# One kernel of attention and mixture of experts: the preparation moves from a block of its own into attention's block

## The chip, the cores and the metric

The kernel runs on one core of one Trainium2 chip. The metric is the device time of one execution in microseconds. The kernel before takes 2116.58 us, the median of three runs between 2116.27 and 2116.94.

## The reference

For 16 batches of 512 tokens with 128 features (float32): six modulation rows come from a conditioning vector, then attention with 16 heads and a mixture of 8 experts, each behind a layer norm that is scaled and shifted by that modulation.

```python
mod = (_silu(c) @ wmod).reshape(B, 6, 1, -1)           # sa, ca, ga, sb, cb, gb
ga = (2 * (ga >= 0) - 1) * jnp.maximum(jnp.abs(ga), 0.25)   # gb likewise
h = _layernorm(x) * (1 + ca) + sa
x = x + ga * attention(h, W_Q, W_K, W_V, W_out, b_out) # causal softmax, 16 heads of 64
h = _layernorm(x) * (1 + cb) + sb
x = x + gb * experts(h, W1, b1, W2, b2, Wr, br)        # top 2 of 8, gelu
```

## The kernel before

The kernel is written as three blocks, one after the other; each block gives every engine its own list of instructions, and all engines meet at a block's end. The first block prepares. SP loads the first batch's x, c, b1, b2, wmod and the raw weights of q, k and v; POOL makes the identity, the mask and a row of -0.5, and loads the biases and the output's weights W_out (L206 to L211). TensorE transposes c, b1 and b2 (L220 to L222), VectorE copies them out (L250 to L252), silu of c is made (ACT L233, VectorE L255 to L257), six products with wmod give the modulation (L226, copied and incremented at L259 and L261), and eight small VectorE operations give the gates (L265 to L268). Each of the four weight matrices is then split in two parts: ACT rounds it to fp32r (hi, L237) and VectorE subtracts (lo, L273), since every product of the kernel is made as hi*hi + lo*hi + hi*lo.

The second block is attention. It handles a batch's 16 heads as eight pairs; the 16 batches are one body written out, a hardware loop of 14 turns, and one body written out. Ahead of the first pair stands a chain for batch 0: statistics (`ln_stats`, VectorE L653 and L657), the inverse deviation on POOL (`inv_std`, L330 and L333), the normalized rows (`ln_apply`, L665), four transposes (`h_transposes`, L383), scale and shift out of PSUM (`h_evac`, ACT L553, which reads the modulation), `round_h` and `rest_h` (ACT L588, VectorE L671), the projections of pair 0 (`project_q`, `project_k`, L357 to L359), their rounding (ACT L561 and L565) and the rests (`rest_q`, `rest_k`, VectorE L676 and L682). Then TensorE's queue holds for each pair, in this order: the scores (L410) in three units, in later pairs the weighted values (L451) and the transposes of the previous pair's probabilities (L436), the projections for the next pair, and two chunks of the values' projection (`values`). VectorE's queue holds the eight masks with their maxima (`mask_and_max`, L701), copies of transposed probabilities (L694), the rests of q and k for the next pair, and the inverse sums (`invert_sums`, L710), which release POOL's normalization (L347). ACT's queue holds the exponentials (L580), roundings, and copies of transposed probabilities and of values (`values_out`, L597).

The raw weights stand in `v_sb`, which the values overwrite from pair 0 (slots 0 and 1) and pair 1 (slots 2 and 3) on; the other temporaries of the preparation stand in `probs`. The third block is the mixture of experts. It uses the gates, b1, b2, Wr and br.

Of the kernel before, what the change touches and what calls it, by code (L numbers as in the profile page):

```python
# [12 lines left out]
P = 128  # L13
# [31 lines left out]
def adaln_moe_kernel(nc, resid, W_Q, W_K, W_V, W_out, b_out, W1, b1, W2, b2, Wr, br, c_in, wmod, out):  # L45
# [10 lines left out]
    with ExitStack() as ctx:  # L56
# [61 lines left out]
        with ExitStack() as pa:  # L118
# [29 lines left out]
            with ExitStack() as ps:  # L148

                raw_w = [v_sb[:, i, :] for i in range(3)]  # L150
                raw_wo = v_sb[:, 3, :]
                zv = probs[:, :, :, :].rearrange("p a b n -> p (a b n)")
                wmod_sb = zv[:, 0:6 * D]
                c_rows = zv[0:B, 1024:1024 + D]
                b1_rows = zv[0:E * HC, 1152:1152 + P]
                b2_rows = zv[0:E, 1600:1600 + D]
                c_cols = zv[:, 1280:1280 + B]
                e_c = zv[:, 1312:1312 + B]
                e1_c = zv[:, 1344:1344 + B]
                sig_c = zv[:, 1376:1376 + B]  # L160
                silu_c = zv[:, 1408:1408 + B]
                g_sign = [zv[:, 1440:1440 + B], zv[:, 1472:1472 + B]]
                g_mag = [zv[:, 1504:1504 + B], zv[:, 1536:1536 + B]]

                flat_w = [tuple(w[:, :] for w in pair_w) for pair_w in (wq, wk, wv)]
                flat_w.append(tuple(w[:, :, :].rearrange("p n d -> p (n d)") for w in wo))

                load_rows = sem("load_rows")
                load_w = [sem(f"load_w_{n}") for n in "qkvo"]
                w_rounded = sem("w_rounded")  # L170
                load_mod = sem("load_mod")
                load_kept = sem("load_kept")
                pool_zero = sem("pool_zero")
                pool_const = sem("pool_const")
                cols_ps = sem("cols_ps")
                exp_c = sem("exp_c")
                dve_chain = sem("dve_chain")
                cols_ok = sem("cols_ok")
                silu_ok = sem("silu_ok")
                mod_ps = sem("mod_ps")  # L180
                gates_ok = sem("gates_ok")

                with nc.Block() as block:
                    @block.sync
                    def _(sp):

                        sp.dma_start(x_all[:, 0:NT, :], resid[0].rearrange("(t p) d -> p t d", p=P)).then_inc(x_in, 16)
                        sp.dma_start(c_rows, c_in).then_inc(load_rows, 16)
                        sp.dma_start(b1_rows, b1.rearrange("e (c p) -> (e c) p", p=P)).then_inc(load_rows, 16)
                        sp.dma_start(b2_rows, b2).then_inc(load_rows, 16)  # L190
                        sp.dma_start(wmod_sb, wmod).then_inc(load_mod, 16)
                        for dst, src, load in zip(raw_w, (W_Q, W_K, W_V), load_w):
                            sp.dma_start(dst, src.rearrange("d h c -> d (h c)")).then_inc(load, 16)
                    @block.gpsimd
                    def _(pool):
                        pool.memset(ident[:, :], 0.0).then_inc(pool_zero, 1)
                        pool.memset(mask_w[:, :], 0.0).then_inc(pool_zero, 1)
                        pool.memset(neg_half[:, :], -0.5).then_inc(pool_const, 1)
                        pool.wait_ge(pool_zero, 2)
                        pool.affine_select(out=ident[:, :], in_=ident[:, :], compare_op=ALU.not_equal, fill=1.0,  # L200
                                           base=0, pattern=[[-1, P]], channel_multiplier=1).then_inc(pool_const, 1)

                        pool.affine_select(out=mask_w[:, 384:512], in_=mask_w[:, 384:512], compare_op=ALU.is_ge,
                                           fill=NEG, base=0, pattern=[[-1, P]], channel_multiplier=1)\
                            .then_inc(pool_const, 1)
                        pool.dma_start(bo_col[:, :], b_out.rearrange("(d o) -> d o", o=1)).then_inc(load_kept, 16)  # L206
                        pool.dma_start(br_b[:, :], br.partition_broadcast(P)).then_inc(load_kept, 16)
                        pool.dma_start(wr_sb[:, :], Wr).then_inc(load_kept, 16)
                        wo_v = W_out.rearrange("c (n two) d -> two c n d", two=2)
                        for half in range(2):  # L210
                            pool.dma_start(raw_wo[half * DH:(half + 1) * DH, :].rearrange("p (n d) -> p n d", n=NP),  # L211
                                           wo_v[half]).then_inc(load_w[3], 16)
                        pool.wait_ge(load_kept, 48)

                    @block.tensor
                    def _(pe):

                        pe.wait_ge(pool_const, 3)
                        pe.wait_ge(load_rows, 48)
                        pe.transpose(g_bank[:, 0:B], c_rows, ident[0:B, 0:B])  # L220
                        pe.transpose(g_bank[:, B:B + E * HC], b1_rows, ident[0:E * HC, 0:E * HC])
                        pe.transpose(g_bank[:, 64:64 + E], b2_rows, ident[0:E, 0:E]).then_inc(cols_ps, 1)  # L222
                        pe.wait_ge(silu_ok, 1)
                        pe.wait_ge(load_mod, 16)
                        for j in range(6):
                            mm = pe.matmul(s_banks[0][:, j * B:(j + 1) * B], wmod_sb[:, j * D:(j + 1) * D], silu_c,  # L226
                                           start=True, stop=True)
                        mm.then_inc(mod_ps, 1)

                    @block.scalar  # L230
                    def _(act):
                        act.wait_ge(cols_ok, 3)
                        act.activation(e_c, c_cols, ACT.Exp, scale=-1.0).then_inc(exp_c, 1)  # L233

                        for (hi, lo), raw, load, n in zip(flat_w, raw_w + [raw_wo], load_w, (1, 1, 1, 2)):
                            act.wait_ge(load, 16 * n)
                            act.activation(hi, raw, ACT.Copy).then_inc(w_rounded, 1)  # L237

                    @block.vector
                    def _(dve):  # L240
                        done = [0]

                        def link(ins):

                            done[0] += 1
                            ins.then_inc(dve_chain, 1)
                            dve.wait_ge(dve_chain, done[0])
# [64 lines left out]
            with nc.Block() as block:  # L312
# [41 lines left out]
                def _(pe):  # L354
# [130 lines left out]
                    def body(b, first, last):  # L485
# [4 lines left out]
                        for p in range(NP):  # L490
# [32 lines left out]
                            if now:  # L523
                                values(b, p, 0, now[0])
# [744 lines left out]
```

## Time and profile before

| what | us |
|---|---|
| median of three runs | 2116.58 |
| the profiled execution | 2116.83 |
| its span | 2115.0 |
| first block, up to the first instruction of the second | 19.5 |
| chain of batch 0, up to the first scores | 11.7 |
| attention, 16 batches | about 1318 |
| experts, 16 batches | about 766 |

The profile is of one execution. Times in the views are microseconds from the span's start. In a timeline row the first number is the start, the second the time taken, and in brackets stands how long the engine had been idle before and what released it. "PEld" is TensorE's load of weights beside the product. Matmul ends are modelled, so that the time between starts says more than the time of one.

### The profile page before, as it was taken

The numbers are of one execution on the slowest core, as the hardware profiler recorded it, in microseconds if no ns is written. First come the engines' busy times: TensorE is split into PE (matmuls) and PEld (weight loads), VectorE is DVE, ScalarE is ACT, GpSimd is POOL, SyncE is SP. The second block draws the span as 40 slices with busy tenths as digits, with TensorE's granted clock in tenths as the row PEclk, the third lists the DMA queues.
The fourth block names the chain that finished last, engine by engine and source line by source line (L and its number), as shares of the span: only waits on it lengthen the run. The fifth ranks groups of instructions, "written<-read, shape, count | busy, mean of one in ns | idle before, by whom it ended". The sixth has DMA issues, their size and how long they took to land. (4 is left out here: it accounts for less than half of the span.)

```text
span 2115.0 us, 46428 instructions
## 1 busy us (share of the span) xinstructions
PE 2016.3 (95%) x12751; PEld 1556.6 (74%) x12751; DVE 1691.4 (80%) x4517; ACT 1535.3 (73%) x3749; POOL 722.1 (34%) x1215
## 2 busy tenths in 40 slices
PE   4999999999999999999999999799999999999998
PEld 3777777777777776777777777478888888888887
DVE  5878777778778778778787787599888888988887
ACT  4878778778778777777777787477777777777775
POOL 2434443344443444343443443122222222222222
PEclk9999999999999999999999999899999999999999
DMA  3000000000000000000000000311111121111111
GB/s 108 21 1 1 0 0 0 0 0 0 0 0 0 0 0 0 0 0 0 0 0 0 0 1 1 113 48 51 45 45 45 56 69 50 50 45 45 45 59 37
DMA packets 41933, 49.46 MB, mean 23 GB/s; under 512 B 3177, under 2 KB 23713, under 8 KB 41889
## 3 DMA queue, kind: packets, MB, share of 16 engines
q1 hardware_dynamic: 41632, 48.41, 7.3%
q0 software_dynamic: 256, 0.53, 0.2%
q8 instruction: 20, 0.33, 0.1%
q14 instruction: 25, 0.20, 0.0%
HBM read 44.47 MB, written 4.46 MB: 23 GB/s over the span
## 5 line engine op out<-in xcount | busy, mean ns | idle before, releaser
L347 POOL TENSOR_SCALAR probs<-probs,rdenom 128x512 f32<-128x512 f32 (+3 forms) x1024 | 522.4, 532 | 742.3 <-DVE rdenom L710 742.3
L580 ACT ACTIVATE probs<-probs,neg_max 128x512 f32<-128x512 f32 (+3 forms) x1024 | 561.8, 550 | 204.8 <-DVE neg_max L701 204.8
L1027 ACT ACTIVATE hidden<-banks,b_cols 128x512 f32<-128x512 f32 x512 | 348.4, 685 | 198.5 <-PE banks L893 174.8
L701 DVE CUSTOM_DVE_ANT_0 probs<-banks,mask_w 128x512 f32<-128x512 f32 (+3 forms) x1024 | 433.5, 487 | 52.5 <-PE banks L410 50.5
L1146 DVE TENSOR_TENSOR hid_lo<-hidden,hid_hi 128x512 fp32r<-128x512 f32 x512 | 386.7, 763 | 67.7 <-ACT hid_hi L1035 55.4
L694 DVE COPY probs_T<-banks 128x512 f32<-128x512 f32 x384 | 262.2, 683 | 151.5 <-PE banks L436 149.6
L436 PE MATMUL banks<-ident,probs 128*128 128x128 f32 x2560 | 348.6, 275 | 0.5 <-DVE z_lo L714 0.5
L436 PEld LDWEIGHTS banks<-ident,probs 128*128 128x128 f32 x2560 | 293.4, 141 | 52.4 <-DVE neg_max L701 12.0
L965 POOL TENSOR_TENSOR acc<-acc,y_w 128x512 f32<-128x512 f32 x112 | 155.1, 1385 | 489.6 <-DVE y_w L1159 489.6
L451 PE MATMUL banks<-probs_T,v_sb 128*64 128x512 f32 (+3 forms) x2048 | 303.9, 439 | 10.4 <-DVE neg_max L701 5.4
L451 PEld LDWEIGHTS banks<-probs_T,v_sb 128*64 128x64 f32 x2048 | 139.1, 136 | 157.9 <-issue 123.3
L410 PE MATMUL banks<-k_hi,q_hi 64*128 64x512 f32 (+3 forms) x1024 | 184.4, 349 | 41.1 <-DVE k_lo L682 28.3
L891 PE MATMUL banks<-h_hi,w_hi 128*128 128x512 f32 x512 | 207.3, 405 | 3.6 <-DVE w_lo L1132 2.6
L904 PE MATMUL banks<-hid_hi,w_hi 128*128 128x512 f32 x512 | 199.9, 390 | 1.9 <-DVE w_lo L1132 1.9
L893 PE MATMUL banks<-h_lo,w_hi 128*128 128x512 f32 x512 | 201.0, 393 | 0.0
L892 PE MATMUL banks<-h_hi,w_lo 128*128 128x512 f32 x512 | 200.4, 391 | 0.0
L905 PE MATMUL banks<-hid_hi,w_lo 128*128 128x512 f32 x512 | 199.9, 390 | 0.0
L906 PE MATMUL banks<-hid_lo,w_hi 128*128 128x512 f32 x512 | 199.8, 390 | 0.0
L580 ACT ACTIVATION_READ_ACCUMULATOR probs<-probs,neg_max 128x1 f32 x1024 | 192.6, 188 | 0.0
L410 PEld LDWEIGHTS banks<-k_hi,q_hi 64*128 64x128 f32 x1024 | 100.4, 184 | 104.6 <-issue 69.4
L410 PE MATMUL banks<-k_hi,q_lo 64*128 64x512 f32 (+3 forms) x1024 | 169.6, 318 | 0.0
L410 PE MATMUL banks<-k_lo,q_hi 64*128 64x512 f32 (+3 forms) x1024 | 169.5, 319 | 0.0
(138 smaller groups left out, 3408.0 us busy)
## 6 DMA issues: line engine op xcount, KB each, us to landing
w_rows<-w_kept SPq DMA_DIRECT2D x128, 256.0 KB, 4.0
x_all<-in_L_attn_resid_dram SPq DMA_DIRECT2D x16, 256.0 KB, 2.8
out_dram<-y_result SPq DMA_DIRECT2D x16, 256.0 KB, 2.3
w_raw<-in_L_ffn_W_dram SPq DMA_DIRECT2D x12, 256.0 KB, 3.9
hidden<-in_L_ffn_W_dram SPq DMA_DIRECT2D x4, 256.0 KB, 5.8
v_sb<-in_L_attn_W_Q_dram SPq DMA_DIRECT2D x1, 512.0 KB, 5.2
v_sb<-in_L_attn_W_K_dram SPq DMA_DIRECT2D x1, 512.0 KB, 8.0
v_sb<-in_L_attn_W_V_dram SPq DMA_DIRECT2D x1, 512.0 KB, 11.4
```

Of the source, the lines that this page charges most:

```text
L347: pool.tensor_scalar(part, part, rdenom[:, p % 2, 4 * h + r:4 * h + r + 1], 1.0, ALU.mult, ALU.mult)\
L410: mm = pe.matmul(S_BANK[u][h][:, at:at + n], q[own, p % 2, rows], k[own, p % 2, 0:n], start=start, stop=stop)
L436: mm = pe.transpose(T_BANK[u][:, at:at + P], probs[:, p % 2, h, src:src + P], ident[:, :])
L451: mm = pe.matmul(z_bank[h * DH:(h + 1) * DH, c * P:S], v_sb[:, c, hc:hc + DH], probs_T[:, h, KEY_AT[c]:KEY_AT[c] + n], start=(c == 0), sto ...
L580: act.activation(part, part, ACT.Exp, bias=neg_max[:, p % 2, col:col + 1], scale=-1.0, accum_out=denom[:, p % 2, col:col + 1]).then_inc(p_ ...
L694: dve.tensor_copy(dst, src).then_inc(t_dve, 1)
L701: dve.tensor_tensor_reduce(out=probs[:, p % 2, h, at:at + n], in0=S_BANK[u][h][:, col:col + n], in1=mask_w[:, 512 - n:512], scale=-SCALE, ...
L891: pe.matmul(banks[:, c, :], w1_hi[:, e, cols], h2_hi[:, :], start=True, stop=False)
L892: pe.matmul(banks[:, c, :], w1_lo[:, e, cols], h2_hi[:, :], start=False, stop=False)
L893: pe.matmul(banks[:, c, :], w1_hi[:, e, cols], h2_lo[:, :], start=False, stop=True)\
L1027: act.activation(hidden[:, e % 2, c, :], banks[:, c, :], ACT.Gelu, bias=b1_cols[:, e * HC + c:e * HC + c + 1]).then_inc(hid, 1)
L1146: dve.tensor_tensor(hid_lo[:, e % 2, c, :], full, hi.bitcast(F32), ALU.subtract)\
```

## The change

The first block is gone and its instructions stand at the head of attention's lists, in another order. SP issues c first, then x, wmod, the weights of q, k and v, and b1 and b2 last. POOL makes its constants, then the inverse deviation of batch 0, and issues its DMAs behind that. TensorE transposes c, then the normalized rows, then makes the modulation, then the projections of pair 0, and then transposes b1 and b2. ACT rounds q's weights ahead of `h_evac`, k's behind `round_h`, v's behind `round_k`, and the output's at the end of pair 0. VectorE takes silu between the statistics and the normalized rows, and splits q's and k's weights ahead of `rest_h` and `rest_q`; in pair 0 it splits v's weights and makes the gates behind the masks, and splits the output's weights behind the inverse sums. New waits hold TensorE: for the b columns between the first two units of pair 0's scores, and ahead of the values in pair 0 and pair 1 for three and four split matrices. The temporaries move to the half of `probs` that pair 1 is the first to use. The core of the diff:

```diff
-                zv = probs[:, :, :, :].rearrange("p a b n -> p (a b n)")
...
-                with nc.Block() as block:
...
+            zv = probs[:, 1, :, :].rearrange("p b n -> p (b n)")
...
@@ sync
+                    sp.dma_start(c_rows, c_in).then_inc(load_c, 16)
+                    sp.dma_start(x_all[:, 0:NT, :], resid[0].rearrange("(t p) d -> p t d", p=P)).then_inc(x_in, 16)
+                    sp.dma_start(wmod_sb, wmod).then_inc(load_mod, 16)
+                    for dst, src, load in zip(raw_w, (W_Q, W_K, W_V), load_w):
+                        sp.dma_start(dst, src.rearrange("d h c -> d (h c)")).then_inc(load, 16)
+                    sp.dma_start(b1_rows, b1.rearrange("e (c p) -> (e c) p", p=P)).then_inc(load_b, 16)
+                    sp.dma_start(b2_rows, b2).then_inc(load_b, 16)
                     batches(sp, body)
@@ gpsimd
...
+                    pool.wait_ge(pool_const, 1)
                     inv_std(0)
+                    wo_v = W_out.rearrange("c (n two) d -> two c n d", two=2)
...
+                    pool.wait_ge(load_kept, 48)
@@ tensor, body
-                        if first:
-                            h_transposes(0)
-                            project_q(0, 0)
-                            project_k(0, 0)
...
                             scores(b, p, 0, begin, young)
+                            if begin:
+                                pe.wait_ge(b_ok, 1)
                             scores(b, p, 2, begin, young)
...
+                            if first and p < 2:
+                                pe.wait_ge(w_split, 3 + p)
                             if now:
                                 values(b, p, 0, now[0])
@@ tensor, ahead of the batches
+                    pe.wait_ge(pool_const, 3)
+                    pe.wait_ge(load_c, 16)
+                    pe.transpose(g_bank[:, 0:B], c_rows, ident[0:B, 0:B]).then_inc(c_ps, 1)
+                    h_transposes(0)
+                    pe.wait_ge(silu_ok, 1)
+                    pe.wait_ge(load_mod, 16)
+                    for j in range(6):
+                        mm = pe.matmul(s_banks[0][:, j * B:(j + 1) * B], wmod_sb[:, j * D:(j + 1) * D], silu_c,
+                                       start=True, stop=True)
+                    mm.then_inc(mod_ps, 1)
+                    pe.wait_ge(w_split, 1)
+                    project_q(0, 0)
+                    pe.wait_ge(w_split, 2)
+                    project_k(0, 0)
+                    pe.wait_ge(load_b, 32)
+                    pe.transpose(g_bank[:, B:B + E * HC], b1_rows, ident[0:E * HC, 0:E * HC])
+                    pe.transpose(g_bank[:, 64:64 + E], b2_rows, ident[0:E, 0:E]).then_inc(b_ps, 1)
@@ scalar
+                    def round_weights(i):
+                        (hi, lo), raw, load = flat_w[i], (raw_w + [raw_wo])[i], load_w[i]
+                        act.wait_ge(load, 32 if i == 3 else 16)
+                        act.activation(hi, raw, ACT.Copy).then_inc(w_rounded, 1)
+
+                    act.wait_ge(c_ok, 1)
+                    act.activation(e_c, c_cols, ACT.Exp, scale=-1.0).then_inc(exp_c, 1)
+                    round_weights(0)
+                    act.wait_ge(mod_ok, 1)
                     h_evac(0)
                     round_h(0)
+                    round_weights(1)
                     round_q(0, 0, False)
                     round_k(0, 0)
+                    round_weights(2)
...
                             if len(now) > 1:
                                 values_out(b, 1, now[1])
+                            if begin:
+                                round_weights(3)
@@ vector
+                    def split_weights(i):
+                        (hi, lo), raw = flat_w[i], (raw_w + [raw_wo])[i]
+                        dve.wait_ge(w_rounded, i + 1)
+                        dve.tensor_tensor(lo, raw, hi.bitcast(F32), ALU.subtract).then_inc(w_split, 1)
+
+                    def gates():
...
+                    dve.wait_ge(c_ps, 1)
+                    dve.tensor_copy(c_cols, g_bank[:, 0:B]).then_inc(c_ok, 1)
                     ln_stats(0)
+                    dve.wait_ge(exp_c, 1)
+                    link(dve.tensor_scalar(e1_c, e_c, 1.0, None, ALU.add))
+                    link(dve.reciprocal(sig_c, e1_c))
+                    dve.wait_ge(c_ok, 1)
+                    dve.tensor_tensor(silu_c, c_cols, sig_c, ALU.mult).then_inc(silu_ok, 1)
                     ln_apply(0)
+                    dve.wait_ge(mod_ps, 1)
+                    link(dve.tensor_copy(mod_cols[:, :, :].rearrange("p j b -> p (j b)"), s_banks[0][:, 0:6 * B]))
+                    link(dve.tensor_scalar(mod_cols[:, 4, :], mod_cols[:, 4, :], 1.0, None, ALU.add))
+                    dve.tensor_scalar(mod_cols[:, 1, :], mod_cols[:, 1, :], 1.0, None, ALU.add).then_inc(mod_ok, 1)
+                    split_weights(0)
                     rest_h(0)
+                    split_weights(1)
                     rest_q(0, 0)
                     rest_k(0, 0)
+                    dve.wait_ge(b_ps, 1)
+                    dve.tensor_copy(b1_cols[:, :], g_bank[:, B:B + E * HC])
+                    dve.tensor_copy(b2_cols[:, :], g_bank[:, 64:64 + E]).then_inc(b_ok, 1)
...
                             mask_and_max(b, p, 1, 1)
+                            if begin:
+                                split_weights(2)
+                                gates()
...
                             invert_sums(b, p)
+                            if begin:
+                                split_weights(3)
```

## Rows read from the trace of the kernel before

**Rows 1.** The page, parts 1 and 3: busy time; packets, MB, share of a queue.

```profile
PE 2016.3 (95%) x12751; PEld 1556.6 (74%) x12751; DVE 1691.4 (80%) x4517; ACT 1535.3 (73%) x3749; POOL 722.1 (34%) x1215
...
q8 instruction: 20, 0.33, 0.1%
```

**Rows 2.** Windows: one batch; width, busy us (instructions) by engine, clock, DMA share, GB/s.

```profile
216.27:298.18 81.91, 78.81 (x586) 58.68 (x585) 63.25 (x199) 61.78 (x179) 33.86 (x66) 1.00 0.00 0
```

**Rows 3.** Timeline: attn_T of batch 0 and of batch 13, made one batch later.

```profile
134.31 0.81 DVE L723 TENSOR_SCALAR attn_T<-banks,bo_col,gate_cols 128x512 f32<-128x512 f32 x1 [4.62 <-PE banks L472]
...
1199.23 0.81 DVE L723 TENSOR_SCALAR attn_T<-banks,bo_col,gate_cols 128x512 f32<-128x512 f32 x1 [4.86 <-PE banks L472]
```

**Rows 4.** DMA view, 0 to 40 us: count, KB, median us from issue to landing.

```profile
x_all<-in_L_attn_resid_dram SPq DMA_DIRECT2D x8, 256.0 KB, 2.7
...
v_sb<-in_L_attn_W_V_dram SPq DMA_DIRECT2D x1, 512.0 KB, 11.4
```

**Rows 5.** Timeline, first block: start, us, engine, line, operation, [idle before <-releaser].

```profile
0.74 0.44 SPq L187 DMA_DIRECT2D x_all<-in_L_attn_resid_dram  x1
...
1.24 0.49 SPq L188 DMA_DIRECT2D probs<-in_L_c_dram  x1
...
4.25 0.25 PE L220 MATMUL banks<-ident,probs 16*128 16x16 f32 x1 [4.25 <-DMA probs<-in_L_ffn_b_dram]
...
6.73 2.71 PE L226 MATMUL banks<-probs 128*128 128x16 f32 x12 [2.02 <-DMA probs<-in_L_wmod_dram]
8.31 1.06 ACT L237 ACTIVATE wq_hi<-v_sb 128x1024 fp32r<-128x1024 f32 x1 [2.98 <-DMA v_sb<-in_L_attn_W_Q_dram]
9.47 0.26 DVE L259 COPY mod_cols<-banks 128x96 f32<-128x96 f32 x1 [3.43 <-PE banks L226]
9.77 0.38 DVE L261 TENSOR_SCALAR mod_cols<-mod_cols 128x16 f32<-128x16 f32 x2
...
11.61 1.22 DVE L273 TENSOR_TENSOR wq_lo<-v_sb,wq_hi 128x1024 fp32r<-128x1024 f32 x1
```

**Rows 6.** Timeline, second block up to the first scores.

```profile
19.56 0.87 DVE L653 BATCH_NORM_STATS2 stats<-x_all 128x6 f32<-128x128 f32 x4 [0.53 <-PEq L183]
...
21.19 1.04 POOL L333 TENSOR_TENSOR rstd<-var_eps,neg_half 128x4 f32<-128x4 f32 x1
22.27 1.11 DVE L665 TENSOR_SCALAR xn<-x_all,meanvar,rstd 128x128 f32<-128x128 f32 x4 [1.55 <-POOL rstd L333]
...
23.44 1.12 PE L383 MATMUL banks<-ident,xn 128*128 128x128 f32 x4 [14.00 <-DVE xn L665]
24.59 0.78 ACT L553 ACTIVATE hf<-banks,mod_cols 128x512 f32<-128x512 f32 x1 [7.20 <-PE banks L383]
...
26.81 0.79 PE L357 MATMUL banks<-h_hi,wq_hi 128*128 128x512 f32 x1 [2.26 <-DVE h_lo L671]
...
28.25 0.63 PE L357 MATMUL banks<-h_hi,wk_hi 128*128 128x512 f32 x1
...
31.24 0.50 PE L410 MATMUL banks<-k_hi,q_hi 64*128 64x512 f32 x2 [1.50 <-DVE k_lo L682]
```

**Rows 7.** Timeline, end of pair 0 and start of pair 1.

```profile
37.10 0.69 DVE L676 TENSOR_TENSOR q_lo<-banks,q_hi 128x512 fp32r<-128x512 f32 x1 [1.36 <-ACT q_hi L561]
...
38.43 1.06 ACT L597 ACTIVATE v_sb<-banks 128x512 f32<-128x512 f32 x2
38.56 0.69 DVE L682 TENSOR_TENSOR k_lo<-banks,k_hi 128x512 fp32r<-128x512 f32 x1 [0.77 <-ACT k_hi L565]
...
39.36 0.50 PE L410 MATMUL banks<-k_hi,q_hi 64*128 64x512 f32 x2 [1.90 <-issue]
...
40.47 0.69 DVE L701 CUSTOM_DVE_ANT_0 probs<-banks,mask_w 128x512 f32<-128x512 f32 x1 [1.11 <-PE banks L410]
```

**Rows 8.** Windows, columns as in Rows 2: two stretches of pair 1.

```profile
40.40:43.75 3.35, 3.35 (x24) 3.13 (x21) 3.28 (x15) 2.54 (x9) 3.23 (x7) 0.50 0.29 83
43.75:48.08 4.33, 4.33 (x27) 3.53 (x27) 2.92 (x7) 4.33 (x14) 0.44 (x1) 0.99 0.23 66
```

More of the change, by code:

```diff
@@ new lines, in adaln_moe_kernel @@
+            raw_w = [v_sb[:, i, :] for i in range(3)]
+            raw_wo = v_sb[:, 3, :]
+            zv = probs[:, 1, :, :].rearrange("p b n -> p (b n)")
+            wmod_sb = zv[:, 0:6 * D]
+            c_rows = zv[0:B, 1024:1024 + D]
+            b1_rows = zv[0:E * HC, 1152:1152 + P]
+            b2_rows = zv[0:E, 1600:1600 + D]
+            c_cols = zv[:, 1280:1280 + B]
+            e_c = zv[:, 1312:1312 + B]
+            e1_c = zv[:, 1344:1344 + B]
+            sig_c = zv[:, 1376:1376 + B]
@@ new lines, in adaln_moe_kernel @@
+            silu_c = zv[:, 1408:1408 + B]
+            g_sign = [zv[:, 1440:1440 + B], zv[:, 1472:1472 + B]]
+            g_mag = [zv[:, 1504:1504 + B], zv[:, 1536:1536 + B]]
+            flat_w = [tuple(w[:, :] for w in pair_w) for pair_w in (wq, wk, wv)]
+            flat_w.append(tuple(w[:, :, :].rearrange("p n d -> p (n d)") for w in wo))
+            load_c, load_b = sem("load_c"), sem("load_b")
+            load_w = [sem(f"load_w_{n}") for n in "qkvo"]
+            w_rounded = sem("w_rounded")
@@ new lines, in adaln_moe_kernel @@
+            load_mod = sem("load_mod")
+            load_kept = sem("load_kept")
+            pool_zero = sem("pool_zero")
+            pool_const = sem("pool_const")
+            c_ps, b_ps = sem("c_ps"), sem("b_ps")
+            exp_c = sem("exp_c")
+            dve_chain = sem("dve_chain")
+            c_ok = sem("c_ok")
+            silu_ok = sem("silu_ok")
+            mod_ok = sem("mod_ok")
+            mod_ps = sem("mod_ps")
+            gates_ok = sem("gates_ok")
+            b_ok = sem("b_ok")
@@ L277, in adaln_moe_kernel @@
+            w_split = sem("w_split")
             qk_ps = sem("qk_ps")
@@ new lines, in gates @@
+                    def gates():
+                        for g, j in enumerate((2, 5)):
+                            raw, sign, mag = mod_cols[:, j, :], g_sign[g], g_mag[g]
+                            link(dve.tensor_scalar(sign, raw, 0.0, 2.0, ALU.is_ge, ALU.mult))
+                            link(dve.tensor_scalar(sign, sign, 1.0, None, ALU.subtract))
+                            link(dve.tensor_tensor(mag, raw, sign, ALU.mult))
+                            dve.scalar_tensor_tensor(out=gate_cols[:, g, :], in0=mag, scalar=GATE_MIN, in1=sign,
+                                                     op0=ALU.max, op1=ALU.mult).then_inc(gates_ok, 1)
```

127 lines of the change are left out of this document (20 added, 107 removed).

## The prediction

> **What bounds the kernel now.** I read the page first. TensorE is busy for 95% of the span [rows 1], so over the whole the kernel is bound by TensorE, and the windows of one batch of the loop say the same: 78.81 of 81.91 us [rows 2]. attn_T is written at 134.31 and, 13 turns of the loop later, at 1199.23 [rows 3], 81.92 us apart each time, so a batch does not depend on how the first one began. What is gained or lost ahead of the loop then reaches the end one for one. The change touches only what stands ahead of the loop and two pairs of the first batch, so the average says nothing on its price, and I read the timeline of that stretch.
>
> The first block has three things in a row in it. The loads: the last of the v weights lands 11.4 us after its issue, at about 15.4 [rows 4]. The modulation: its products run from 6.73 to 9.44, and the columns are ready at 9.77 + 0.38 = 10.15 [rows 5]. The splits: four times 1.22 us on VectorE [rows 5], of which the last two wait for v's load. The second block starts at 19.56 with the statistics, which need only x. x was issued at 0.74 [rows 5] and an x load takes 2.7 us [rows 4], so it had lain there since about 3.5. That is 16 us of waiting for nothing, and it is what the change can reach. From 19.56 a chain with no slack follows, in which every engine waits for the one before [rows 6], up to the first scores at 31.24: 11.7 us.
>
> **Up to the first scores.** I lay the chain of [rows 6] at the time when its inputs are there.
> - c is now first in SP's queue (issue at 0.74 in place of 1.24). Its landing is not shown alone; TensorE started on it at 4.25 only because it waited for b2 as well [rows 5], so with the 0.5 us by which it moves up 3.7 is an upper bound, and the transpose and the copy (0.17) fit ahead of x.
> - x is second: issue 1.24, landing 2.7 later, 3.95. Statistics start at about 4.05 in place of 19.56: 15.5 us earlier. Then POOL's rstd at 5.7, xn at 22.27 - 15.5 = 6.8, transposes from 7.95 to 9.05. The three silu operations stand in VectorE's queue between statistics and xn; VectorE idles 1.55 us there [rows 6] and they took 0.67 in the first block, so they are free.
> - TensorE makes the modulation behind the transposes: 9.05 + 2.71 [rows 5] = 11.8. Before, this ran beside other work; now it is in the chain. wmod had landed by 6.73 from a later place in the queue [rows 5], so its load is not what is late. Copy and the two increments: 10.15 - 9.47 = 0.68, so `h_evac` starts at 12.55 in place of 24.59. The lead shrinks from 15.5 to 12.0 us.
> - ACT has q's rounding (1.06) in front of `h_evac`. It started at 8.31 on q's landing [rows 5], so it ends by 9.4, 3 us ahead of time. VectorE splits q from 12.5 to 13.7; `rest_h` takes some 0.7 us, as a rest of 512 columns does [rows 7], ahead of the 26.81 at which q's products start [rows 6], so it is due at 26.06 - 12.0 = 14.0. Free.
> - k's rounding follows `round_h` on ACT, which ends where `rest_h` starts, at 14.0: so k is rounded at 15.1 and split at 16.4. `project_k` would be due at 28.25 - 12.0 = 16.2 [rows 6]. It waits 0.1 to 0.2 us: 0.15.
> - v's rounding (1.06) runs from 18.5 to 19.6 on ACT, ahead of the first exponential, which cannot be due before the first mask, some 1.1 us behind the first scores (40.47 - 39.36 in pair 1 [rows 7]). The b transposes take less than the 1.5 us that TensorE idles between `project_k` and the scores [rows 6]; the b copies (0.35 us on VectorE behind `rest_k`) are done 0.7 us ahead of the first mask. b1 and b2 stand behind v's weights in the queue, which land by 15.4 [rows 4]; TensorE gets to them at 17.9. Free, with 2 us of margin.
>
> Scores start at 31.24 - 12.0 + 0.15 = 19.4: **11.85 us earlier**. Bounds: x or c half a us later or earlier; if the two increments and waits cost nothing more, 12.5, if each of some ten new hand-overs costs 0.1 us more than counted, 10.9.
>
> **Pair 0 and pair 1** (in times of before, to be shifted). VectorE ends its masks at 37.10 - 1.36 = 35.74 [rows 7]. Split of v's weights, 1.23: 36.97. Gates, eight operations between the increments' end at 10.15 and the first split at 11.61 [rows 5], so 1.46, and some more for the split's wait, 1.5: 38.5. The rest of q, which ran at 37.10, is 1.4 late and ends at 39.2. The rest of k was due at 38.56 [rows 7], now 39.2 to 39.9, and the scores of pair 1 start 0.65 late, at 40.0. The values' products wait for the split and move 1.25 us back into TensorE's idle stretch before 39.36 (1.90 us [rows 7]); ACT's copies of them, which ended at 39.49 [rows 7], end 0.1 late. ACT then rounds the output's weights, 39.6 to 40.65, and VectorE splits them until 41.9. So the first mask of pair 1 starts at 41.95 in place of 40.47 [rows 7]: 1.5 us late on VectorE and ACT. TensorE is not held by that in full. In 40.40 to 43.75 its clock was granted at half, 1.2 GHz, and VectorE was busy 3.28 of the 3.35 us; from 43.75 to 48.08 TensorE and ACT are both full [rows 8]. VectorE has 1.4 us of idle time in the second stretch, which takes up some of the 1.5 us; I estimate that 0.9 reach the scores of pair 2. The bounds are 0.6 (only TensorE's lateness counts) and 1.5 (ACT's in full). I take **0.9**, nearer to the lower end, since TensorE, late by 0.65, is as full as ACT.
>
> Here the trace and a page weigh differently. The trace shows the clock at half for 3.35 us behind TensorE's idle 1.90 us [rows 7, 8], at a place where VectorE covered it. The Trainium skill ("TensorE: Matmul & The Clock Gate", section "What's actually happening") has a throttled default that activity lifts and idling brings back. By it, the change, which lengthens the waits of pair 0, invites the low level and may put it in another place. This agrees with the row; what it would do is the second rival.
>
> **Behind that** nothing changes: gates, b1 and b2 are read by later parts only, and the loop is the same. The next x loads follow b2 in SP's queue, beside the output's weights, which have until about 27.7. The meeting of the engines at 19.5 disappears inside the 15.5 us already counted.
>
> **Sum** against the profiled execution: 2116.83 - 11.85 + 0.9 = 2105.9. It lies 0.25 us above the median of the runs, so 2105.6 in terms of the median.
>
> **Rivals.**
> 1. *VectorE becomes the bound of the first pairs.* All of what is put in its queue counts: 1.23 + 1.5 + 1.23 + 0.35 = 4.3 us in place of 0.9. For it: VectorE's masks release both ACT and the transposes. Against: 1.36 + 0.77 us of idle time [rows 7]. 2116.6 - 11.85 + 4.3 = 2109.0. Chance 0.10.
> 2. *The clock falls in another place*, over the scores of pair 0 or over pair 2, where TensorE is full. 3.35 us at half [rows 8] do 1.7 us of work, so 1.7 us more: 2107.3. Chance 0.10.
> 3. *The b columns hold the scores.* TensorE stands at `load_b` with all scores behind it, and the output's weights take a share of the DMA. If b lands 4 us behind where v's did, at 19.4, the transposes, copies and second unit come some 1.5 us late: 2107.1. Against: everything ahead of it in the queue landed by 15.4 [rows 4], and the output's weights, which shared the DMA then, now start later. Chance 0.05.
> 4. *The first pairs take the added work for nothing*: 2104.7. Chance 0.08.
> 5. *The reordering does not do what it says*: x shares the DMA with what follows and lands with the last of the weights, at 15.4. Then the chain starts 4.1 us earlier and not 15.5, and with 0.9 lost the time is 2113.4, within 0.2%. Against: the 2.7 us of an x load [rows 4]. Chance 0.02.
> 6. *Slower: the turn of the loop costs more.* The loop's instructions stand at other addresses now, so a turn could meet a fetch that it does not meet today. There are 14 turns in each of the loops; TensorE's idle time in a whole batch is 81.91 - 78.81 = 3.1 us [rows 2], and a stall of up to that size per turn is conceivable. From 15.2 / 14 = 1.1 us per turn the kernel is over 0.2% slower; at 1.2 us per turn it takes 2105.6 + 16.8 = 2122.4. Against: 20 packets of instructions in the whole execution [rows 1], so no turn fetches today. The Trainium skill ("Runtime: NRT & Kernel Launch", section "Instruction fetch mechanics") says that a taken branch whose target is out of the window forces a fetch; no row here shows one. Chance 0.015.
>
> **How the numbers follow.** The forecast, 2105.6, has 0.63, with a range of its own of 2104.9 to 2106.8 by the bounds above. Rivals 1 to 3 lie above it, rival 4 below it. The range from 2104.0 to 2109.0 leaves out rivals 5 and 6, half of rival 1, and some of rivals 2 and 4. A measurement of this kernel can tell about 0.2%, 4.2 us, from no change; below 2112.35 is faster. The forecast and rivals 1 to 4 give 0.96 for faster; rival 5 and what joins several mishaps 0.025; rival 6 0.015.
>
> **What the profile will show.** Right: one block; statistics at about 4, xn at 6.8, modulation products 9 to 11.8, hf at 12.55, first scores at 19.4, first mask of pair 1 at 41.95 - 11.85 = 30.1, first attn_T at 134.31 - 10.95 = 123.4, and 81.9 us between batches. Rival 1: attn_T at 126 or later and VectorE never idle from pair 0's masks to pair 2. Rival 2: a low clock in the windows elsewhere than in pair 1. Rival 3: TensorE idle before L220 to L222's b transposes, released by a DMA. Rival 5: statistics late behind a DMA. Rival 6: batches longer than 81.91. I would be wrong above all if the modulation in the chain costs more than its 2.71 + 0.68 us, or if the delay of pair 1 does not fade.

## The result

The changed kernel takes 2191.68 us (median of six runs, 2190.68 to 2193.58), the kernel before 2116.76 in the same session. The ratio is 1.0354, with an interval of 1.034 to 1.0367: 3.5% slower, where 0.5% faster was forecast.

From the page of the changed kernel (parts 1, 3 and 5; in part 5 the last column is the engine's idle time before the group and what ended most of it):

```profile
span 2189.9 us, 46415 instructions
...
PE 2046.3 (93%) x12751; PEld 1568.1 (72%) x12751; DVE 1687.3 (77%) x4517; ACT 1536.3 (70%) x3749; POOL 725.5 (33%) x1215
...
q14 instruction: 89, 0.73, 0.1%
...
L667 DVE CUSTOM_DVE_ANT_0 probs<-banks,mask_w 128x512 f32<-128x512 f32 (+3 forms) x1024 | 433.4, 487 | 106.4 <-issue 62.2
```

From the page of the kernel before (parts 3 and 5):

```profile
q14 instruction: 25, 0.20, 0.0%
...
L701 DVE CUSTOM_DVE_ANT_0 probs<-banks,mask_w 128x512 f32<-128x512 f32 (+3 forms) x1024 | 433.5, 487 | 52.5 <-PE banks L410 50.5
```

TensorE's share fell from 95% [rows 1] to 93% with the same 12751 products, so most of the 75 us is idle time of TensorE. Its busy time rose by 30 us, which comes up again below. Two lines stand out. Queue q14, instructions, carries 89 packets in place of 25. And the masks on VectorE are idle for 106.4 us in place of 52.5, of which 62.2 are put down to "issue", which means that VectorE waited for nothing that semaphores show; before, that group waited for TensorE.

The starts of attn_T, the same two as in [rows 3]:

```profile
123.28 0.81 DVE L689 TENSOR_SCALAR attn_T<-banks,bo_col,gate_cols 128x512 f32<-128x512 f32 x1 [4.98 <-PE banks L407]
...
1275.54 0.81 DVE L689 TENSOR_SCALAR attn_T<-banks,bo_col,gate_cols 128x512 f32<-128x512 f32 x1 [4.98 <-PE banks L407]
```

The first is 11.0 us earlier than the 134.31 of before, as forecast (123.4). The second is 76.3 us later than 1199.23. Between them lie 13 returns of the loop: (1275.54 - 123.28) / 13 = 88.64 us each, in place of 81.92. The whole loss is here: 13 x 6.72 = 87.4 us.

The start of the changed kernel, which answers to [rows 5] and [rows 6] (timeline):

```profile
2.63 0.26 PE L473 MATMUL banks<-ident,probs 16*128 16x16 f32 x1 [2.63 <-DMA probs<-in_L_c_dram]
...
4.09 0.87 DVE L619 BATCH_NORM_STATS2 stats<-x_all 128x6 f32<-128x128 f32 x4 [0.99 <-DMA x_all<-in_L_attn_resid_dram]
...
6.75 1.18 DVE L631 TENSOR_SCALAR xn<-x_all,meanvar,rstd 128x128 f32<-128x128 f32 x4 [0.96 <-POOL rstd L249]
...
7.98 1.12 PE L318 MATMUL banks<-ident,xn 128*128 128x128 f32 x4 [5.10 <-DVE xn L631]
...
8.89 2.58 PE L478 MATMUL banks<-probs 128*128 128x16 f32 x12
...
12.22 0.78 ACT L506 ACTIVATE hf<-banks,mod_cols 128x512 f32<-128x512 f32 x1 [2.48 <-DVE mod_cols L732]
...
14.53 0.76 PE L292 MATMUL banks<-h_hi,wq_hi 128*128 128x512 f32 x1 [3.06 <-DVE h_lo L637]
...
19.07 0.79 PE L345 MATMUL banks<-k_hi,q_hi 64*128 64x512 f32 x2 [1.20 <-DVE k_lo L648]
```

The chain is the forecast one within 0.4 us: statistics at 4.09 (forecast 4.05), xn at 6.75 (6.8), scale and shift at 12.22 (12.55), scores at 19.07 (19.4).

Pair 0's end and pair 1's start, which answer to [rows 7]:

```profile
24.19 1.22 DVE L709 TENSOR_TENSOR wv_lo<-v_sb,wv_hi 128x1024 fp32r<-128x1024 f32 x1
...
27.89 1.06 ACT L555 ACTIVATE wo_hi<-v_sb 128x1024 fp32r<-128x1024 f32 x1
...
28.13 0.50 PE L345 MATMUL banks<-k_hi,q_hi 64*128 64x512 f32 x2 [1.01 <-DVE q_lo L642]
...
28.98 1.22 DVE L709 TENSOR_TENSOR wo_lo<-v_sb,wo_hi 128x1024 fp32r<-128x1024 f32 x1 [0.84 <-ACT wo_hi L555]
...
30.13 0.68 DVE L667 CUSTOM_DVE_ANT_0 probs<-banks,mask_w 128x512 f32<-128x512 f32 x1
```

Scores of pair 1 at 28.13 (forecast 40.0 - 11.85 = 28.15), first mask at 30.13 (30.1).

Then the turn of the loop. First the changed kernel's timeline at the first return of the loop, then VectorE's row at the same place before:

```profile
177.14 0.23 PE L345 MATMUL banks<-k_hi,q_hi 64*128 64x128 f32 x2
...
180.66 0.69 DVE L667 CUSTOM_DVE_ANT_0 probs<-banks,mask_w 128x512 f32<-128x512 f32 x1 [4.77 <-issue]
...
182.04 1.35 PE L386 MATMUL banks<-probs_T,v_sb 128*64 128x512 f32 x4 [4.46 <-DVE neg_max L667]
```

```profile
197.51 0.69 DVE L701 CUSTOM_DVE_ANT_0 probs<-banks,mask_w 128x512 f32<-128x512 f32 x1 [0.31 <-PE banks L410]
```

TensorE has the scores of the next batch's first pair in PSUM before 178. VectorE's first mask of the turn starts at 180.66, 4.77 us after the end of its previous operation and for no semaphore; before, it waited 0.31 us for the scores. TensorE stands behind it (4.46 us, until the maxima are there), and so does ACT. The DMA view of one turn of the changed kernel (265 to 353.7 us), queue of instructions, with packets and MB:

```profile
q14 instruction: 5, 0.04, 0.2%
```

Five packets of 8 KB in each turn; the same view of the kernel before, between 218 and 400 us, has none. At the return that begins this turn VectorE stands from 263.6 to 268.4 us, but for a few register instructions in between. Two packets start in that stretch, at 264.0 and 266.5, a third behind it at 269.1, the next at 300.7 and 327.2, and the fifth of the view at 352.6, where the next return begins. Over the 13 returns 13 x 5 = 65 packets are what 89 has over 24. So the loop's code is fetched anew in each turn; that it is VectorE's code is what runs 1 and 2 show.

After the stall TensorE's clock is low as well (windows of 2 us; width, busy us (instructions) of TensorE, its weight loads, VectorE, ACT, POOL, then granted clock):

```profile
266.00:268.00 2.00, 0.00 (x0) 0.00 (x0) 0.00 (x0) 0.00 (x0) 1.01 (x3) 1.00 0.02 4
268.00:270.00 2.00, 0.21 (x2) 0.21 (x4) 1.59 (x7) 0.85 (x3) 0.00 (x0) 0.51 0.02 4
270.00:272.00 2.00, 2.00 (x6) 0.56 (x6) 1.79 (x10) 2.00 (x7) 0.00 (x0) 0.50 0.00 0
272.00:274.00 2.00, 2.00 (x12) 0.95 (x8) 0.00 (x0) 0.25 (x2) 0.00 (x0) 0.50 0.00 0
...
276.00:278.00 2.00, 2.00 (x14) 1.68 (x13) 1.80 (x4) 2.00 (x7) 0.00 (x0) 1.00 0.00 0
...
268.30:275.00 6.70, 5.21 (x21) 2.47 (x21) 3.38 (x16) 3.73 (x12) 0.00 (x0) 0.51 0.01 1
```

TensorE stands idle in the first window, works at half clock (1.2 GHz) in the next three, and is back at 2.4 GHz in the fifth. So of 6.7 us per turn, 4.77 - 0.31 = 4.5 are the stall, and the other 2.2 go with the stretch at half clock behind it. No run removes the second share alone, but two figures have its size. In the last row TensorE is busy for 5.2 us at half clock, work that takes half of that at full, so I estimate up to 2.6 us. And the busy time of TensorE, for the same 12751 products, is 2046.3 us here and 2015.3 in run 1 below, which has no such stall: 31.0 / 13 = 2.4 us per return.

### The profile page after: what moved, and what is told of

Its sections match the earlier page's. It is cut to its first block and busy times, and to the rows that moved or that the text cites. A ratio compares the mean times of both kernels' runs of the same rounds, so it can differ in the third digit from the quotient of the medians.

```text
span 2189.9 us, 46415 instructions
## 1 busy us (share of the span) xinstructions
PE 2046.3 (93%) x12751; PEld 1568.1 (72%) x12751; DVE 1687.3 (77%) x4517; ACT 1536.3 (70%) x3749; POOL 725.5 (33%) x1215
## 3 DMA queue, kind: packets, MB, share of 16 engines
HBM read 44.47 MB, written 4.46 MB: 22 GB/s over the span
## 5 line engine op out<-in xcount | busy, mean ns | idle before, releaser
L667 DVE CUSTOM_DVE_ANT_0 probs<-banks,mask_w 128x512 f32<-128x512 f32 (+3 forms) x1024 | 433.4, 487 | 106.4 <-issue 62.2
L386 PE MATMUL banks<-probs_T,v_sb 128*64 128x512 f32 (+3 forms) x2048 | 331.4, 469 | 64.8 <-DVE neg_max L667 59.8
L371 PE MATMUL banks<-ident,probs 128*128 128x128 f32 x2560 | 353.3, 278 | 1.9 <-DVE neg_max L667 1.4
L386 PEld LDWEIGHTS banks<-probs_T,v_sb 128*64 128x64 f32 x2048 | 147.4, 145 | 229.5 <-issue 196.8
```

What stands on the lines that cost most here:

```text
L371: mm = pe.transpose(T_BANK[u][:, at:at + P], probs[:, p % 2, h, src:src + P], ident[:, :])
L386: mm = pe.matmul(z_bank[h * DH:(h + 1) * DH, c * P:S], v_sb[:, c, hc:hc + DH], probs_T[:, h, KEY_AT[c]:KEY_AT[c] + n], start=(c == 0), sto ...
L667: dve.tensor_tensor_reduce(out=probs[:, p % 2, h, at:at + n], in0=S_BANK[u][h][:, col:col + n], in1=mask_w[:, 512 - n:512], scale=-SCALE, ...
```

## The experiments

**Theory F**: the place of VectorE's loop in its list decides. In the compiled programs the loop of attention has 362 instructions on VectorE, waits among them; the traces record as many from one attn_T to the next. It starts at instruction 323 of VectorE's list before and at 317 after the change, since the meeting of the engines and some waits of the first block are gone. The starts are counted in the compiled programs, and no trace shows them. **Rival R**: the longer turn comes from the rhythm in which the engines enter the loop, or from another part of the change.

Waits that are already met move the loop and do no work. Each puts one instruction into the list (a step of 0.07 us in the traces, where VectorE idles for c). The edit, for eight, on VectorE behind its first wait:

```diff
                     dve.wait_ge(c_ps, 1)
+                    for _ in range(8):
+                        wait_alone(dve, c_ps, 1)
                     dve.tensor_copy(c_cols, g_bank[:, 0:B]).then_inc(c_ok, 1)
```

Runs 1 and 11 were timed several times, the others once.

**Run 1, eight waits on VectorE.**

> The changed kernel with eight waits that are already met put into VectorE's list ahead of the loop (behind the arrival of c, where VectorE idles). The work is the same; attention's loop of VectorE starts at instruction 325 of its list in place of 317 (323 before the change). Theory F (place of the loop's instructions: a turn of VectorE's loop needs its code fetched anew): the fetches of every turn go away, turns are 81.9 us again, time 2105.5 to 2107.5 us, and the instruction queue q14 has about 25 packets in place of 89. Rival R (the turns are longer because the engines run in another rhythm after the new start, or through another part of the change): the pad changes nothing, 2190 to 2193 us, and 89 packets.

Measured: 2105.01 us (2104.63 to 2105.35), ratio 0.9944 to the kernel before, interval 0.9928 to 0.9961. Page, and the two attn_T:

```profile
span 2103.2 us, 46423 instructions
...
PE 2015.3 (96%) x12751; PEld 1556.2 (74%) x12751; DVE 1688.9 (80%) x4517; ACT 1534.8 (73%) x3749; POOL 722.5 (34%) x1215
...
q14 instruction: 24, 0.20, 0.0%
```

```profile
123.06 0.81 DVE L689 TENSOR_SCALAR attn_T<-banks,bo_col,gate_cols 128x512 f32<-128x512 f32 x1 [4.63 <-PE banks L407]
...
1188.32 0.81 DVE L689 TENSOR_SCALAR attn_T<-banks,bo_col,gate_cols 128x512 f32<-128x512 f32 x1 [4.87 <-PE banks L407]
```

24 packets, and (1188.32 - 123.06) / 13 = 81.94 us per turn. Eight instructions that do nothing take off 86.7 us. Theory F stands, rival R falls.

**Run 2, the same waits on ACT** (behind its wait for `c_ok`).

> The changed kernel with the same eight met waits in ACT's list instead, where ACT idles; VectorE's list is as in the changed kernel. Theory F says that VectorE's place alone matters, since the long idle time called issue stands on VectorE: 2190 to 2193 us and 89 packets in q14. If any shift of code or of time ahead of the loop did it (rival R, rhythm), or if ACT's code were fetched, the time would move: to 2106 us.

Measured: 2190.23 us, 89 packets. A shift of another engine's list does nothing.

**Run 3, the kernel before with forty waits on VectorE**: start at 363.

> The kernel before with forty met waits in VectorE's list in its first block, where it idles for c: VectorE's loop starts at instruction 363 in place of 323, and nothing else differs. Theory F: a loop of 362 instructions that starts late in a block of code touches one block more, so the kernel before takes on the loss of the changed one, about 14 turns x 6.8 us less part of it: 2190 to 2215 us with some 85 to 90 packets in q14. Rival R: 2117 to 2119 us, since the pad costs 40 x some 0.05 us at most.

Measured: 2162.48 us, 89 packets. A loss with the same 89 packets can be put upon the kernel before with none of the change in it. It is 45.6 us, less than the expected 73 or more, and 1.2 us of it are the forty waits' own (attn_T of batch 0 starts at 135.5 in place of 134.3). The waits of VectorE between 200 and 1250 us (us in total, times, longest) of this kernel:

```profile
DVE probs L703 <- PE banks L412: 55.4, 82, 2.6
DVE probs L703 <- issue: 10.8, 4, 2.8
```

The longest is 2.8 us and not 5. At the other returns the wait is put down to TensorE's scores, with 2.6 us as the longest, but the scores had been there. The timeline at one of them, TensorE's last product of the first mask's scores and that mask:

```profile
274.03 0.40 PE L412 MATMUL banks<-k_lo,q_hi 64*128 64x512 f32 x2
...
276.55 0.69 DVE L703 CUSTOM_DVE_ANT_0 probs<-banks,mask_w 128x512 f32<-128x512 f32 x1 [2.55 <-PE banks L412]
```

One packet starts during that wait, at 274.4 us, and the next behind it, at 276.8. At each of the 13 returns of this run VectorE's first instruction of the turn, of whatever kind, comes 2.2 to 2.4 us late, once; in the changed kernel it stands twice at each return, for 2.1 to 2.4 us each. My reading, from the geometry: where the start lies well inside its block of code, one fetch is waited for at the return and the next one arrives in time; where it lies at the end of a block, as at 317, the block behind it is needed at once and two fetches are waited for.

**Run 4, the kernel before with eight waits**: start at 331.

> As the run before, but with eight waits: VectorE's loop starts at instruction 331. Theory F with blocks of 8 KB (128 instructions of 64 bytes, my reading of the packets) and room for the loop in a band of some 23 start positions: 331 is still inside, 2116.5 to 2117.5 us, 25 packets. If only the exact place of before was good, about 2195 us. Rival R: 2117 us.

Measured: 2117.06 us, 24 packets, no change. The good place is wider than one start.

**Runs 5, 6, 9 and 10, the edges of the band**: the changed kernel with 22, 29, 3 and 26 waits.

> The changed kernel with 22 met waits on VectorE ahead of the loop: it starts at instruction 339 of VectorE's list. The good starts seen are 323, 325 and 331, the bad ones 317 and 363. Theory F with numbers: code is fetched in packets of 8 KB, which is 128 instructions of 64 bytes, the five fetches of a bad turn are four touched blocks and the one behind them, and four blocks stay. A loop of 362 instructions then stays when it touches three blocks, so for 23 starts in a row, the first of which lies between 318 and 323. 339 is inside the band for each of these: 2105 to 2107 us, 24 packets. Rival: the band is narrower or has another cause (for instance blocks of another size): 2140 us or more and about 89 packets.

> The same with 29 waits: start at 346, which is one past the last start that the band of 23 allows, wherever its first start lies in 318 to 323. Theory F: 89 packets again and 2140 to 2165 us, less than the changed kernel's 2190, since the start then lies 23 to 28 instructions into its block and only one fetch of 2.5 us is waited for at the branch, as in the run with 40 waits. Rival, a band that reaches further up: 2105 to 2107 us and 24 packets.

> The changed kernel with three met waits on VectorE ahead of the loop, start at 320: the lower edge of the band lies somewhere in 318 to 323. Theory F allows both outcomes and each fixes the upper edge, since the band is 23 starts wide: if 320 is good (2105 to 2107 us, 24 packets), the upper edge is 340 to 342 and the run with 26 waits (343) must be bad; if 320 is bad (2185 to 2192 us, 89 packets: two fetches of 2.5 us at the branch, as at 317), the upper edge is 343 to 345 and 343 must be good. Both good or both bad speaks against blocks of 128 instructions with room for four.

> The same with 26 waits, start at 343; see the run with three. Good if that is bad (2104.5 to 2106 us, 24 packets), bad if that is good (2150 to 2165 us, 89 packets).

| start of VectorE's loop | kernel | packets in q14 | us |
|---|---|---|---|
| 317 | changed | 89 | 2191.68 |
| 320 | changed, 3 waits | 89 | 2191.54 |
| 323 | before | 25 | 2116.76 |
| 325 | changed, 8 waits | 24 | 2105.01 |
| 331 | before, 8 waits | 24 | 2117.06 |
| 339 | changed, 22 waits | 25 | 2104.72 |
| 343 | changed, 26 waits | 24 | 2104.96 |
| 346 | changed, 29 waits | 89 | 2159.38 |
| 363 | before, 40 waits | 89 | 2162.48 |

The waits of VectorE with the start at 320 and at 346, columns as above:

```profile
DVE probs L667 <- issue: 59.3, 12, 5.2
```

```profile
DVE probs L667 <- issue: 35.2, 12, 3.1
```

About 5 us per return just below the band, about 3 just above it, as the geometry says. All four outcomes are as expected. The lower edge lies in 321 to 323 and the upper in 343 to 345, so the band is 21 to 25 starts wide. A loop of 362 instructions that may touch three blocks of n instructions has 3n - 361 good starts: n = 128 gives 23, n = 127 gives 20, n = 129 gives 26. The width alone would also allow other numbers of blocks, for instance six of 64; the packets decide. With blocks of 128 a loop in a bad place touches four, and four with one fetched ahead make the five packets of a turn; with blocks of 64 it would be eight. So a block is 128 instructions, and a packet of 8 KB carries one. The reading that fits all nine starts: three touched blocks and the one fetched ahead of them stay; with a fourth touched block the turn fetches all five.

**Run 7, the gates later**, on top of run 1's eight waits.

```diff
                                 split_weights(2)
-                                gates()
...
                             if begin:
+                                gates()
+                                dve.wait_ge(gates_ok, 2)
                                 split_weights(3)
```

> The changed kernel with eight met waits, and the gates' eight operations moved from ahead of the rest of q (pair 0) to behind the inverse sums, in front of the split of the output's weights. It tests the step on pair 0 and pair 1. By the prediction the gates delay the rest of q by 1.4 us and the scores of pair 1 by 0.65 us; moved, pair 1's scores start some 0.6 us earlier (27.5 in place of 28.1), but the split of the output's weights comes later by up to 1 us, so that pair 1's first mask gains nothing: 2104.6 to 2105.4 us against 2105.0. Rival, TensorE alone sets pair 1: 2104.0 to 2104.4 us.

Measured: 2107.39 us, 2.4 slower than run 1, outside both. For a single time that is little, but the profile has it too: attn_T of batch 0 is at 126.28, 3.2 us behind run 1's. Timeline of the run, and two windows (columns as before):

```profile
26.96 0.50 PE L345 MATMUL banks<-k_hi,q_hi 64*128 64x512 f32 x2 [0.76 <-issue]
...
27.14 5.06 POOL L282 TENSOR_SCALAR probs<-probs,rdenom 128x512 f32<-128x512 f32 x8 [17.41 <-DVE rdenom L676]
27.25 0.61 DVE L716 TENSOR_TENSOR probs<-mod_cols,probs 128x16 f32<-128x16 f32 x1
...
29.27 0.63 DVE L717 SCALAR_TENSOR_TENSOR gate_cols<-probs 128x16 f32<-128x16 f32 x1
29.93 1.58 DVE L709 TENSOR_TENSOR wo_lo<-v_sb,wo_hi 128x1024 fp32r<-128x1024 f32 x1
31.43 0.68 DVE L667 CUSTOM_DVE_ANT_0 probs<-banks,mask_w 128x512 f32<-128x512 f32 x1
```

```profile
29.00:31.00 2.00, 0.09 (x2) 0.00 (x0) 1.93 (x3) 0.00 (x0) 2.00 (x4) 1.00 0.09 25
31.00:37.80 6.80, 4.84 (x17) 4.20 (x18) 5.09 (x19) 5.65 (x19) 1.20 (x2) 0.50 0.38 115
```

The step on the rest of q holds: pair 1's scores start at 26.96 in place of 28.14. But the gates now run beside POOL's normalization. The four of their eight operations that read two tensors take 0.41 to 0.63 us where they took 0.17 to 0.18 ahead of it; the four that read one tensor take 0.12 to 0.24. The first mask is 1.4 us later than in run 1 (30.01), TensorE has nothing for 2 us, and from 31 to 37.8 its clock is at half. By the profile this is rival 2 of the prediction, a low clock in another place, in a kernel of my own making.

**Run 8, the modulation ahead of the transposes**, again on top of run 1's eight waits.

```diff
-                    h_transposes(0)
                     pe.wait_ge(silu_ok, 1)
...
                     mm.then_inc(mod_ps, 1)
+                    h_transposes(0)
```

> The changed kernel with eight met waits, and the six modulation products ahead of the four transposes in TensorE's list. It tests the step that put 2.6 us of products into the chain. silu is ready at 5.8 us and wmod by about 6.7, the normalized rows at 7.7: the products end at 8.5 to 9.3, the transposes 1.1 us later, at 9.6 to 10.4 in place of 11.3, and the scale and shift no longer wait for the modulation's copies. h is scaled 1.7 to 2.4 us earlier, and the time is 2102.6 to 2103.4 us. Rival, wmod lands later than 6.7 or the rounding of q's weights, which stands ahead in ACT's list, holds it: 2104 to 2105 us.

Measured: 2102.2 us, 2.8 less than run 1 and 0.4 below the range expected; timeline:

```profile
5.67 2.74 PE L477 MATMUL banks<-probs 128*128 128x16 f32 x12 [3.02 <-DVE probs L729]
...
8.25 1.09 PE L318 MATMUL banks<-ident,xn 128*128 128x128 f32 x4
...
8.45 0.26 DVE L732 COPY mod_cols<-banks 128x96 f32<-128x96 f32 x1 [0.71 <-PE banks L477]
...
9.45 0.78 ACT L506 ACTIVATE hf<-banks,mod_cols 128x512 f32<-128x512 f32 x1
```

The products start at 5.67, on silu and not on wmod, which had landed by then. Scale and shift start at 9.45 in place of 12.03 in run 1, 2.6 us earlier; expected were 1.7 to 2.4, since I had the products start only at wmod's landing. What holds them now is q's rounding, ahead of them in ACT's list, which ends at 9.50; the expectation had that as a rival, and it costs little. attn_T of batch 0 is at 120.53, 2.5 us ahead of run 1's. So the 2.6 us of products that the sum had laid into the chain did stand there.

**Run 11, the same kernel in five rounds.**

> The kernel with eight met waits and the modulation's products ahead of the transposes once more, now timed in five rounds: its one time was 2102.2 us, so 2101.8 to 2102.8 us, a ratio of 0.9929 to 0.9935 to the kernel before, if that one time was representative; a rival is that its pair 1 sometimes meets the low clock, which would spread its times up to 2105.

Measured: 2103.01 us (2102.28 to 2103.38), ratio 0.9933, interval 0.9919 to 0.9946. The median lies 0.2 us above the range expected, and the one time of 2102.2 below all five. By the medians 2.0 us of the 2.6 arrive at the end. The rival, a low clock in pair 1, did not come: the spread is 1.1 us. This is the fastest kernel of the study, 13.9 us below the kernel before.

## Why the prediction was wrong

- **What bounds the kernel, the up to 16 us that lie ahead of the loop:** right.
- **Up to the first scores, 11.85 us:** right. 31.24 - 19.07 = 12.2 us were measured. The hand-overs and both splits lay within 0.5 us of where the sum put them; the b columns and the weights' landings held nothing.
- **Pair 0 and pair 1, 0.9 us:** right in size, in part by luck. The scores of pair 1 lead by 39.36 - 28.13 = 11.2 us, so 1.0 us is lost by then where the sum had 0.65, and attn_T of batch 0 leads by 11.0. But 0.6 us of the 1.0 had been lost before the added work began: VectorE's masks of pair 0 end at 24.19 in place of 35.74, a lead of 11.55 after the 12.2 of the scores. The sum has nothing there.
- **The clock** is what the rows show in that place; that all of the 0.6 us is its share was not tested. In run 1 the products of pair 0's scores start 0.56 and 0.43 us apart (rows below, the third starts at 19.87); before, the same products start 0.23 us apart (31.56 and 31.79 in its timeline). A step of 0.43 is what products of this width have in run 7 between 31 and 37.8, at a granted 0.50. The windows of run 1 print 1.00 here only because its trace has no record of the clock ahead of 22.9 us, where one of full clock stands; in the kernel before that record stands at 30.2. So before, the clock had risen by the time of pair 0's scores, and in the changed chain it had not: from their first to their last product pass 22.22 - 18.88 = 3.3 us in place of 33.06 - 31.24 = 1.8. Pair 1 in turn has no low stretch: the windows of run 1 grant the full clock throughout from 25 to 50 us, where [rows 8] has 3.35 us at half. From pair 1's first mask (a lead of 40.47 - 30.13 = 10.3 us) to attn_T (11.0) 0.7 us come back; how much of that is the clock's was not measured. So half of what rival 2 describes happened, over pair 0, without its 1.7 us. The rule that the prediction quotes from the Trainium skill ("TensorE: Matmul & The Clock Gate", section "What's actually happening"), a low default that activity lifts, agrees with the starts of both traces.

```profile
18.88 0.79 PE L345 MATMUL banks<-k_hi,q_hi 64*128 64x512 f32 x2 [1.20 <-DVE k_lo L648]
...
19.44 0.66 PE L345 MATMUL banks<-k_hi,q_lo 64*128 64x512 f32 x2
...
22.22 0.45 PE L345 MATMUL banks<-k_lo,q_hi 64*128 64x128 f32 x2
```

The last product of pair 0's scores before:

```profile
33.06 0.31 PE L410 MATMUL banks<-k_lo,q_hi 64*128 64x128 f32 x2
```

- **"Behind that nothing changes ... and the loop is the same":** this is the step that failed. It put the cost of a turn at no change, 81.9 us, and 88.64 were measured. The instructions of the loop are the same, but 317 is not 323. By the band above, the loop of VectorE fits into what stays on the engine only for 23 of 128 starts, and before the change it stood at most two places above the lower edge. Taking six instructions out ahead of it costs 13 x 6.7 = 87 us, and eight waits that do nothing take them off again (run 1).
- **Rival 6** named the mechanism, a fetch in each turn, and the point of decision (1.1 us per turn), and gave it a chance of 0.015. It went wrong in four places. Its evidence against, 20 packets in q8, was of the wrong queue: the one that moved is q14, 25 to 89. "No turn fetches today" was taken as a sign of safety, though it says nothing on how near the edge is. The count that would have told, 362 instructions against blocks of 128 and a start that the change moves, was not made. The price at which it was put, 1.2 us, was far below the 4.5 us of two fetches in a row and the half clock behind them. And the ceiling of 3.1 us per turn was no ceiling: TensorE's idle time in today's turn says nothing on how long VectorE can stand for a new reason, and 6.7 us were measured.
- **Rivals 1, 3, 4 and 5** did not come about: pair 1 lost 1.0 us and not 4.3 or nothing, the b transposes followed `project_k` at 17.5 us with no wait for a DMA, and the statistics started at 4.09.
- Without that loss the kernel is run 1: 2105.01 us measured against 2105.6 forecast, and 11.85 us below the kernel before against 11.0. The remaining 0.6 us between attn_T's lead (134.31 - 123.06 = 11.25) and the end was not traced.

## What to carry to other kernels

An edit ahead of a hardware loop moves the loop's code, and a loop that just fits can stop fitting: count each engine's instructions in the body and its start, and look at the packets of the instruction queues per turn before and after any such edit. An idle time named "issue" at the first instruction of every turn, with packets in the instruction queue, points to this, and so can a wait put down to an engine that had long been done (run 3). The test is cheap: a few met waits ahead of the loop, which cure it where the loop is short enough to fit at some start, best so many that the start lies in the middle of its band. And work moved ahead of a loop is worth what its chain says, once: 12 us here, against 87 for a fetch in each turn.

## What the runs showed of the hardware

- VectorE's code comes in packets of 8 KB, and by the band and the five packets per turn each holds 128 instructions. A loop that touches three such blocks is kept, one that touches four is fetched anew in every turn, five packets each, with one wait of 2.2 to 2.8 us at the return (starts 346 and 363) or two of 2.1 to 2.5 us (317 and 320). The Trainium skill ("Runtime: NRT & Kernel Launch", section "Instruction fetch mechanics") gives blocks of 16 KiB with 256 instructions, and two of them held. The size of an instruction that this implies, 64 bytes, agrees with the runs, and so does what is held in total by the reading above, 32 KiB in four packets. The block does not: with 256 instructions and both blocks open to the loop the band would, by an estimate from these figures, be 2 x 256 - 361 = 151 starts wide, and 21 to 25 were measured. The Trainium skill's rule that a taken branch out of the held window is a fetch stall agrees, with 4.77 us. Packets of 16 KB do occur in these kernels, in the other instruction queue (q8: 20 packets, 0.33 MB [rows 1]); no run here shows whose code they carry.
- TensorE's stall of about 4.5 us was followed by 6.7 us at half clock (268.3 to 275 in the windows above, at 0.51), and a return cost half as much again as the stall. In run 3, with stalls of at most 2.8 us, a return cost (45.6 - 1.2) / 13 = 3.4 us.
- Small VectorE operations (128x16) that read two tensors took 0.41 to 0.63 us in place of 0.18 while POOL normalized beside them; those that read one took 0.12 to 0.24 (run 7). POOL's eight normalizations of pair 0 took 5.05 us in run 1 and 5.06 in run 7, with a weight split on VectorE beside them, and 4.09 before, without one.
